# Cross-attention and spline FFN in one kernel: down products and two tails moved round the last FFN's replication

## The reference

```
query, key = ctx @ Wq.T + bq, ctx @ Wk.T + bk
attention  = softmax(query @ key.T)
x = x + layernorm(x) @ attention.T
gate_w, up_w, down_w = spline(control points)        # 2048 x 512, 2048 x 512, 512 x 2048
h = layernorm(x)
x = x + (silu(h @ gate_w.T) * (h @ up_w.T)) @ down_w.T
```

## Time and profile before

| | us |
|---|---|
| median of 3 runs | 267.47 |
| lowest, highest | 265.18, 267.57 |
| span of the profiled execution | 265.8 |
| TensorE busy | 247.6 (93%) |
| VectorE, POOL, ScalarE busy | 188.2, 132.2, 123.6 |

### The profile page before, as it was taken

How to read it: one execution, slowest core, us unless ns; L and a number is a source line. 1 busy time by engine, 2 the same in 40 slices (tenths; PEclk the granted TensorE clock), 3 DMA queues, 4 the chain that set the end, 5 groups by cost and what they waited for, 6 DMA issues and landing times.

```text
span 265.8 us, 4144 instructions
## 1 busy us (share of the span) xinstructions
PE 247.6 (93%) x1400; PEld 171.8 (65%) x1400; DVE 188.2 (71%) x332; ACT 123.6 (46%) x206; POOL 132.2 (50%) x138
## 2 busy tenths in 40 slices
PE   7879649999899999999999999999999999599995
PEld 2223136855475868884858788848586888286684
DVE  0598996698778776866788768667887686465533
ACT  3035542325469652336696523366965233254320
POOL 0398717186883831314939313149393131487800
PEclk9968977999999999999999999999999999889999
DMA  6999107000091000022720000227000002200004
GB/s 184 335 427 419 42 16 297 6 0 2 0 353 44 2 1 2 0 79 79 276 118 0 0 0 0 79 79 296 20 0 0 0 0 79 79 2 0 0 2 158
DMA packets 7355, 23.11 MB, mean 87 GB/s; under 512 B 1201, under 2 KB 2481, under 8 KB 5937
## 3 DMA queue, kind: packets, MB, share of 16 engines
q1 hardware_dynamic: 7344, 22.98, 23.1%
HBM read 18.78 MB, written 4.19 MB: 86 GB/s over the span
## 4 chain that ended last, share of the span: by engine, by line
PE 79%; DVE 10%; ACT 3%; DMA 2%; issue 2%; POOL 1%; SPq 1%; DVEq 0%; POOLq 0%
PE bank L1327 12%; PE bank L1330 12%; PE bank L1372 11%; PE bank L1344 6%; PE bank L1174 5%; PE bank L1279 5%; PE bank L1281 5%; PE bank L1280 5%; DVE prod L876 4%; PE bank L1379 3%; PE bank L1236 3%; PE bank L1192 3%; DMA power<-in_g_power 2%; PE bank L1294 1%; PE bank L1356 1%
## 5 line engine op out<-in xcount | busy, mean ns | idle before, releaser
L1124 POOL TENSOR_TENSOR ih<-inter,ones 128x512 fp32r<-128x512 f32 x64 | 65.0, 1042 | 21.5 <-DVE inter L964 21.4
L964 DVE TENSOR_TENSOR inter<-inter,bank 128x512 f32<-128x512 f32 x64 | 43.7, 686 | 18.1 <-ACT inter L776 14.9
L776 ACT ACTIVATE inter<-bank 128x512 f32<-128x512 f32 x64 | 37.9, 598 | 23.7 <-PE bank L1330 23.6
L1372 PEld LDWEIGHTS bank<-d_r,ih 128*128 128x128 f32 x256 | 31.0, 191 | 7.8 <-issue 5.9
L1372 PE MATMUL bank<-d_r,ih 128*128 128x192 f32 x256 | 32.2, 276 | 0.0
L747 ACT ACTIVATE qk<-bank,nmr,rstd 128x512 f32<-128x512 f32 x16 | 12.5, 780 | 36.7 <-PE bank L1281 19.7
L1327 PE MATMUL bank<-xh,gate_r 128*128 128x512 f32 x64 | 27.6, 431 | 1.5 <-DVE zg L956 1.5
L1111 POOL TENSOR_TENSOR xres<-x,ones 128x2048 f32<-128x2048 f32 x4 | 14.4, 3602 | 24.0 <-DMA out<-xres 23.7
L1330 PE MATMUL bank<-zg,up_v 102*128 102x512 f32 x64 | 25.9, 404 | 0.0
L1327 PE MATMUL bank<-xh,up_r 128*128 128x512 f32 x64 | 25.7, 402 | 0.0
L1330 PE MATMUL bank<-zg,gate_v 102*128 102x512 f32 x64 | 25.6, 400 | 0.0
(11 more groups left out here) (108 smaller groups left out, 454.1 us busy)
## 6 DMA issues: line engine op xcount, KB each, us to landing
x<-in_x SPq DMA_DIRECT2D x4, 1024.0 KB, 5.1
xT<-in_xT SPq DMA_DIRECT2D x4, 1024.0 KB, 7.1
out<-xres SPq DMA_DIRECT2D x16, 256.0 KB, 2.1
ctxT<-in_ctxT SPq DMA_DIRECT2D x4, 512.0 KB, 7.6
rd<-in_d_r SPq DMA_DIRECT2D x2, 768.0 KB, 6.1
knots<-in_d_knot SPq DMA_DIRECT2D x1, 1280.0 KB, 11.7
d_coef<-in_d_coef SPq DMA_DIRECT2D x1, 1024.0 KB, 14.6
d_pt<-in_d_node SPq DMA_DIRECT2D x1, 1024.0 KB, 16.0
```

Source lines behind the costliest of these rows:

```text
L776: nc.scalar.activation(inter[:, m], gbank[m % 2][:], ACT.Silu).then_inc(s["silu_done"], 1)
L964: V.tensor_tensor(inter[:, m], inter[:, m], ubank[m % 2][:], ALU.mult).then_inc(s["mult_done"], 1)
L1124: G.tensor_tensor(ih[:, m], inter[:, m], ones[:, 0].broadcast_to([P, TOK]), ALU.mult).then_inc(s["ih_done"], 1)
L1372: mm(in_blocks(obank[t][:], i // CLS), ih[:, m, t * P:(t + 1) * P], d_r[:, i], start=m == 0, stop=False, skip_group_check=True)
```

## The change

Five things change.

1. In the third turn the attention's output products (`xm`) of batch 3 stand ahead of the down products of tiles 1 and 2. The down products of tile 3 and the tails of tiles 2 and 3 are moved into the last FFN: the down products stand between projection and replication, the tails behind the replication. Tile 3's output then goes to bank 5 (`out_bank`), and the last FFN's first up product waits until tile 2 is added (`out_added`).
2. In the third turn the four bn_stats of batch 3's x (`tile_stats`) stand behind the four maxima, and the rest of `stats` behind tile m = 9.
3. x has two buffers, x0 and x1, used in turn. POOL's copy to xres and its semaphore are gone, the FFN's output is added to x in place, and SP fetches the next x when the stores of the batch before are done.
4. Split of x: xh and xl are written in four pieces, and `xm` takes all its products with xh first and those with xl behind them, with a wait for each piece in tile 0.
5. The loop on the engines is written out.

The diff, cut to its core:

```diff
+        def out_bank(b, t):
+
+            return zdbank if (b, t) == (B - 2, NT - 1) else obank[t]
...
             else:
+                st.down(b - 1, 3, range(0, 16))
                 st.replicate(b)
+                for t in range(2, 4):
+                    st.down_tail(b - 1, t)
...
+                if a == B - 1:
+                    for t in range(NT):
+                        st.tile_stats(a, t)
             st.gate_up(b, 8)
             st.gate_up(b, 9, a)
             st.down_basis(b, 0)
...
+            if a == B - 1:
+                st.stats(a)
             st.gate_up(b, 10)
...
-            st.down(b, 1, range(0, 16))
-            if a is not None:
-                st.stats(a)
+            last = a == B - 1
+            if not last:
+                st.down(b, 1, range(0, 16))
+            if a is not None:
+                if not last:
+                    for t in range(NT):
+                        st.tile_stats(a, t)
+                    st.stats(a)
                 st.xm(a, 0)
             st.gather_halves(b)
+            if last:
+                st.mean_shift(a)
+                st.xm(a, 1)
+                st.add_xm(a, 0)
+                st.xm(a, 2)
+                st.down_split(b)
+                for t in range(1, 4):
+                    st.add_xm(a, t)
+                st.xm(a, 3)
+                for t in range(1, 3):
+                    st.down(b, t, range(0, 16))
+                for t in range(2):
+                    st.down_tail(b, t)
+                for t in range(3):
+                    st.norm_t(a, t)
+                    st.cast_t(a, t)
+                st.norm_t(a, 3)
+                st.cast_t(a, 3)
+                return
...
-            with eng.Fori(0, B - 1) as b:
+            for b in range(B - 1):
...
+                sp.dma_start(out[b, t], x[b % 2][:, t]).then_inc(s["out_stored"], 16)
+
+            sp.wait_ge(s["qk_mm"], 2)
+            sp.dma_start(ctxT[:], d["ctxT"][1]).then_inc(s["ctx_in"], 16)
+            for b in range(B - 1):
+                if first(b):
+                    sp.wait_ge(s["res_done"], RES)
+                else:
+                    sp.wait_ge(s["out_stored"], 16 * NT * b)
+                sp.dma_start(x[(b + 1) % 2][:], d["x"][b + 1]).then_inc(s["x_in"], 16)
...
-                    nc.scalar.activation(xh[:], xT[:], ACT.Copy).then_inc(s["xh_done"], 1)
+                    for n in range(NT):
+                        nc.scalar.activation(xh[:, n], xT[:, n], ACT.Copy).then_inc(s["xh_done"], 1)
...
-                    pool.wait_ge(s["res_done"], RES)
-                    pool.wait_ge(s["dv_done"], 1)
-                    pool.wait_ge(s["x1_added"], NT * (b + 1))
-                    pool.wait_ge(s["out_stored"], 16 * NT * b + 1)
-
-                    G.tensor_tensor(xres[:], x[:], ones[:].broadcast_to([P, NT, HID]), ALU.mult).then_inc(s["x1_kept"], 1)
...
                     for n in range(NT):
+                        if t == 0:
+                            pe.wait_ge(s["xh_done"], NT * b + n + 1)
                         mm(abank[t % 2][:], xh[:, n, c], ph[:, n], start=n == 0, stop=False)
                         mm(abank[t % 2][:], xh[:, n, c], pl[:, n], start=False, stop=False)
+                    for n in range(NT):
+                        if t == 0:
+                            pe.wait_ge(s["xsplit_done"], NT * b + n + 1)
                         last = mm(abank[t % 2][:], xl[:, n, c], ph[:, n], start=False, stop=n == NT - 1)
...
+                        if b == B - 1 and (m, n) == (0, 1):
+                            pe.wait_ge(s["out_added"], NT * b - 1)
...
-                        mm(in_blocks(obank[t][:], i // CLS), ih[:, m, t * P:(t + 1) * P], d_r[:, i], start=m == 0, stop=False, skip_group_check=True)
```

## The result

The changed kernel takes 265.0 us (median of 20 runs, 264.17 to 266.28), the kernel before in the same session 267.57 (20 runs, 265.18 to 268.43). The ratio is 0.9911, with a 95% interval of 0.9892 to 0.9929: 0.9% faster. The ratios here leave out executions that took over 1.5% longer than the fastest of the same kernel; the medians are over all runs. The forecast was 265.3, with the range 263.6 to 267.5.

A forecast was written before the change was run, and what follows sets the result against it. TensorE, busy 93% of the span, bounds the kernel, so only its waits and low clock can yield time. 1.85 - 0.15 + 1.63 - 1.2 = 2.13 us off 267.47 gives 265.3 us, range 263.6 to 267.5.

The forecast's parts named there:

- Down and tails round the replication: From the last attention product to the last FFN's first gate product: moved down products and tails gain 1.85 us.
- Earlier arrival and the transposes: Before the last projection: TensorE reaches the transposes 1.77 us earlier, and the projection follows them 0.31 us sooner.
- The 1.4 of idle forecast: Among the last transposes, now without tails between: TensorE idles 1.4 us of the 3.04 us to the projection.
- The wait for out_added: Last FFN, first up product: TensorE waits 0.15 us after the two gate products for VectorE's addition.
- the later gate: Last FFN: the first gate product starts 4.99 us after the projection instead of 4.76, 0.23 us later.
- The clock: Last FFN's first eight gate and up products: without a long hole they run at full clock, gaining 1.63 us.
- The statistics: Third turn, up product of m = 10: bn_stats behind the maxima delay inter's first product; TensorE waits 1.2 us.
- The rest: Dropped xres copy, second x buffer, split in four, order in attention tiles and written-out loops: 0 us.
- 1 and 2, a clock that falls behind bare transposes: Last transposes: a clock dip as long as now gives 267.0 us (chance 0.2), one of 6.40 us gives 268.5 (0.07).
- 3, no stall: Third turn: early statistics stall TensorE not at all or much less; 264.1 us, chance 0.1.
- 4, written-out code pays: Loop turns: fewer register steps and no table load in turns two and three; at 0.5 us per turn 263.8, chance 0.08.
- 5, the dip as an accident of one execution: Clock dip at 231 us belongs to the profiled execution, not the median one; 0.5 us gained, 267.0, chance 0.05.

The follow-up runs named there:

- e1_rest: Changed kernel with down products, tails and statistics put back in the order of the kernel before; 267.69 us, ratio 0.9969 to the kernel before.
- e6_stats_spread: Changed kernel with batch 3's four bn_stats spread out: behind the maxima, m = 11, m = 14 and the split in halves; 264.25 us, ratio 0.9891.
- e3_fill_products: As e1_rest, with six products that nobody reads in each of the two waits of the last FFN; 265.16 us, ratio 0.9894.
- e2_stats_only: As e1_rest, but with the last batch's bn_stats early, behind the four maxima, and its `stats` behind m = 9; 266.26 us, ratio 0.9933.
- e4_fill_transposes: As e1_rest, with 14 transposes that nobody reads in each of the two waits of the last FFN; 265.20 us, ratio 0.9901.
- e8_shift: As e1_rest, with five products that nobody reads ahead of m = 10 of the third turn; 267.17 us, ratio 0.9972.
- e7_holes_filled: As e6_stats_spread, with four tile 2 down products moved among the transposes and two of tile 3 ahead of the projection; 263.57 us, ratio 0.9852.

## Why the prediction was right, point by point

- **Down and tails round the replication, forecast 1.85.** Right in sum. Earlier arrival and the transposes were to give 1.77 + 0.31 = 2.08; e1_rest against e6_stats_spread gives 2.03. Transposes to projection took 3.12 (forecast 3.04; before 3.35), with 0.25 + 0.69 = 0.94 us of idle attributed in the timeline, and 3.12 - 2.18 = 0.94 in the window. The 1.4 of idle forecast was the mis-sized piece: it took the transposes for 1.64 of work (3.04 - 1.4), and they keep TensorE busy 2.18. That did no harm, because ScalarE's copies and not the transposes time the stretch. Projection to gate is 4.97 (forecast 4.99).
- **The wait for out_added, forecast 0.15.** The up product starts 0.26 behind the gate pair's second and the next 0.34 behind it, where 0.23 apart is the rule from 231.65 on: about 0.14. With the later gate the forecast was 0.15 + 0.23 = 0.38; measured are 0.14 + 0.21 (4.97 against 4.76) = 0.35, and the last part is 38.75 in the changed kernel and 38.40 where only the waits were filled, 0.35 again.
- **The clock, forecast 1.63.** 1.58 by e3_fill_products. The clock was 1.00 from the projection on, and the gate and up products reached 0.23 apart.
- **The statistics, forecast -1.2.** -1.17 by e2_stats_only, -1.19 by e6_stats_spread. Its place (m = 10, first product of inter) was the forecast one. The idle shown is only 0.90; the up product starts 1.06 later behind its gate product than in before (1.30 against 0.24), and the product behind it another 0.11 (0.34 against 0.23). The 0.85 idle was cover as estimated: the reciprocal starts 1.43 later in the turn (18.64 against 17.21 behind the projection), where 1.5 was forecast.
- **The rest, forecast 0.** Right behind the first projection: the second turn is 53.12 in both kernels, 53.11 in e1_rest. For the preparation it is not shown. One thing was not foreseen: xl's split in four takes VectorE 3.09 us instead of 2.29 (and xh's ScalarE 2.19 instead of 1.91). It delays nobody, since eight high products stand before the low ones are wanted.

Third turn: forecast 2.08 - 1.2 = 0.88, measured 0.84. Last part: 1.63 - 0.23 - 0.15 = 1.25, measured 1.13.

**The rivals.** 1 and 2, a clock that falls behind bare transposes: not seen. In the changed kernel the clock is 1.00 in the stretch with 2.18 busy of 3.12, and behind it. The rule of the Trainium skill (TensorE: Matmul & The Clock Gate, Part 4: PE-mode transpose) that the full rate does not engage for transposes is not borne out here as far as keeping the clock goes: fourteen of them in each wait kept 1.00 in e4_fill_transposes. No run shows whether transposes alone would raise a low clock. 3, no stall: refuted by 0.90 of idle. 4, written-out code pays: refuted for the turns, which are the same to 0.01 in before and e1_rest. The stall at a taken branch of which the Trainium skill speaks (Runtime: NRT & Kernel Launch, Instruction fetch mechanics) does not show at these loop ends. 5, the dip as an accident of one execution: wrong as put, since most executions of before have the mean clock that goes with it. But four of 23 on the second chip have 0.972 and spans of 263.0 to 264.4, 1.0 to 2.4 us under that session's median span of 265.4, as an execution without it would; these were not profiled. And e2_stats_only and e8_shift show that the waits alone do not decide it.

So one reason was too simple. The prediction said: fill the waits and the clock stays up. That holds (the profiles of e3_fill_products, e4_fill_transposes and every variant with the cover). Its reverse, that these waits bring the clock down, holds only at the place in time where before has them. It follows that of the 1.63 us a part could have been had with the waits left as they are, in some executions. What sets that place stays open: the runs tell it apart from the statistics, not what the chip looks at.

**Also open:** 2.57 us between the medians against 1.99 behind the first projection. The rest, some 0.6, must lie in the preparation or in executions of either kernel that were not profiled. Up to the first projection the profiled executions of before, the changed kernel and the eight variants spread over 64 to 67 us with nearly the same instructions there, and the low clock lies in other slices from one to the next. Three of the ten have a lower clock there, and theirs are the three longest preparations: the changed kernel (66.16), e3_fill_products (66.52) and e1_rest (67.27) have a mean granted clock of 0.86 over the first 60 us, the other seven 0.89. Before, then the changed kernel:

```profile
0.00:60.00 60.00, 49.80 (x192) 25.25 (x193) 44.73 (x82) 21.25 (x36) 32.11 (x33) 0.89 0.52 191
0.00:60.00 60.00, 50.38 (x188) 25.46 (x189) 44.36 (x83) 21.52 (x39) 30.09 (x33) 0.86 0.52 191
```

Since the other nineteen executions of the changed kernel have a higher mean clock than the profiled one, the 0.69 us that its preparation took longer is probably not what the median has. That does not explain the 0.6, for which the preparation would have to be shorter than before's; the ratio of e1_rest leaves room for it, but it was not measured. The same kind of remainder stands between the variants: e2_stats_only is 1.43 us under e1_rest by the medians, where the turns and the last part give 0.48. So 265.0 lies close to the forecast of 265.3 in part by chance, since no term of the sum stands for this remainder.

## What to carry to other kernels

A block of products that must run anyway is worth most where it covers a chain that nothing else covers: 16 down products and six tail products, moved into two waits, gave 2.0 us in the turn that they left, for 0.35 in the one that they came to, and 1.6 us of clock. Work that is moved early on an in-order engine costs what exceeds the idle time at its new place, and one piece at a time in each of several gaps can cost nothing (e6_stats_spread against the changed kernel: 1.19 us). After a move, look for the holes that it opened, and give them a few pieces of the block (e7_holes_filled: another 0.67 us).

## What the runs showed of the hardware

- Two waits of 1.53 and 1.47 us with TensorE busy 0.69 of 3.67 were followed by a granted clock of 0.52 to 0.54 for some 3.5 us in before and e1_rest, and by 1.00 in e2_stats_only and e8_shift, where the same waits fell 1.1 to 1.2 us later behind the first projection. One profile with or without a dip is no proof of what a wait does to the clock.
- Transposes of 128x128 in fp32, 14 in each wait and nothing else there, kept the granted clock at 1.00.
- An elementwise operation of 128x2048 in four pieces, each with a wait of its own for ScalarE's piece, took VectorE 0.80 us longer than in one (3.09 against 2.29), ScalarE's copy 0.28 (2.19 against 1.91).
